# A pre-norm MoE, attention, MoE block: token lists compared in 16 bits, first gathers and first weight splits moved, first layer by slot halves

## The reference, cut to what matters

```
x = x + 0.5 * ffn(layernorm(x), Wg, w1, w2)
x = x + attention(layernorm(x), w_qkv, w_o)      # 16 heads, causal
x = x + 0.5 * ffn(layernorm(x), Wg, w1, w2)

def ffn(x):                                       # x: 2048 tokens x 256
    probs = softmax(x @ Wg); gates, experts = top_k(probs, 2)
    pos = position of each (token, choice) pair in its expert's list, kept = pos < C
    dispatched = x[list of each expert]           # 8 experts x C slots
    h = relu(dispatched @ w1)                     # 256 -> 1024
    out = h @ w2                                  # 1024 -> 256
    return sum over the two choices of gate * out, back at the token's row
```

## Time and profile before

| what | value |
|---|---|
| time, median of 3 runs (lowest, highest) | 876.12 us (874.57, 880.39) |
| profiled execution: span, first to last instruction | 872.3 us |
| busy in that span: PE, PEld, DVE, ACT, POOL | 88%, 77%, 52%, 42%, 36% |
| mean granted TensorE clock | 0.948 of full |
| first phase: list begins, first layer begins | 37.86 us, 60.21 us |
| third phase begins, list begins, first layer begins | 577.9 us, 605.22 us, 628.65 us |

### The profile page before, as it was taken

One profiled execution on the slowest core, in us unless ns is written; L12 is line 12 of the kernel. 1 busy time (PEld: TensorE's weight loads), 2 busy tenths in 40 slices (PEclk: granted clock), 3 DMA queues, 4 the chain that ended last, 5 costly groups with the idle time before them and its releaser, 6 DMA issues. The chain is left out here.

```text
span 872.3 us, 15775 instructions
## 1 busy us (share of the span) xinstructions
PE 765.8 (88%) x6076; PEld 670.4 (77%) x6076; DVE 452.7 (52%) x848; ACT 369.6 (42%) x611; POOL 310.6 (36%) x363
## 2 busy tenths in 40 slices
PE   5789999999999558888788787776899999999995
PEld 3479999999999546555556554454699999999995
DVE  7755544544453056757655667256554445444630
ACT  4215534554453001546553646523154445444531
POOL 3164364446422452132221212201644644464223
PEclk9899999999999877889988999978999999999998
DMA  9334454245401223220121120052344542554112
GB/s 333 105 119 119 108 148 124 64 118 144 126 9 18 25 96 146 75 76 20 58 77 58 45 75 27 26 164 57 91 119 133 142 125 48 142 137 124 18 18 24
DMA packets 60070, 80.27 MB, mean 92 GB/s; under 512 B 11140, under 2 KB 46980, under 8 KB 59988
## 3 DMA queue, kind: packets, MB, share of 16 engines
q1 hardware_dynamic: 44660, 60.35, 20.6%
q0 software_dynamic: 15360, 19.23, 11.9%
HBM read 51.72 MB, written 19.01 MB: 81 GB/s over the span
## 5 line engine op out<-in xcount | busy, mean ns | idle before, releaser
L610 DVE SCALAR_TENSOR_TENSOR first_h_lo<-first_ps_h,first_h_hi 128x320 fp32r<-128x320 f32 x128 | 62.9, 492 | 104.5 <-ACT first_h_hi L469 104.5
L610 DVE SCALAR_TENSOR_TENSOR second_h_lo<-second_ps_h,second_h_hi 128x320 fp32r<-128x320 f32 x128 | 62.9, 491 | 104.6 <-ACT second_h_hi L469 104.6
L386 POOL DMA_INDIRECT after_first<-first_scaled,first_add_now x40 | 69.4, 1734 | 115.6 <-ACT first_scaled L462 113.0
L386 POOL DMA_INDIRECT out_dram<-second_scaled,second_add_now x40 | 69.2, 1729 | 116.1 <-ACT second_scaled L462 113.5
L1100 DVE TENSOR_REDUCE at_maxima<-at_ps_front 128x4 f32<-128x512 f32 (+2 forms) x96 | 96.3, 1038 | 15.9 <-PE at_ps_front L1228 15.4
L984 POOL TENSOR_SCALAR_AFFINE_SELECT at_probs<-at_probs 128x512 f32<-128x512 f32 x64 | 39.9, 635 | 170.8 <-ACT at_probs L1040 169.9
L1040 ACT ACTIVATE at_probs<-at_ps_keys 128x768 f32<-128x768 f32 (+1 forms) x96 | 81.6, 876 | 25.1 <-PE at_ps_keys L1259 23.5
L721 PE MATMUL first_ps_o<-first_w_hi,first_h_hi 128*128 128x256 f32 x320 | 91.2, 285 | 0.0
L721 PE MATMUL second_ps_o<-second_w_hi,second_h_hi 128*128 128x256 f32 x320 | 91.2, 285 | 0.0
L721 PE MATMUL first_ps_o<-first_w_lo,first_h_hi 128*128 128x256 f32 x320 | 90.0, 281 | 0.0
L721 PE MATMUL first_ps_o<-first_w_hi,first_h_lo 128*128 128x256 f32 x320 | 90.0, 281 | 0.0
(11 more groups left out here) (271 smaller groups left out, 1765.0 us busy)
## 6 DMA issues: line engine op xcount, KB each, us to landing
first_w_raw<-in_L_ffn_w_dram SPq DMA_DIRECT2D x16, 1024.0 KB, 8.6
second_w_raw<-in_L_ffn_w_dram SPq DMA_DIRECT2D x16, 1024.0 KB, 7.1
at_q_stack<-at_pre_hi SPq DMA_DIRECT2D x16, 256.0 KB, 2.4
at_k_stack<-at_pre_hi SPq DMA_DIRECT2D x16, 256.0 KB, 2.5
x<-_attn_hidden_states_dram SPq DMA_DIRECT2D x4, 512.0 KB, 5.6
normed_rows<-first_xn SPq DMA_DIRECT2D x4, 512.0 KB, 6.7
x<-after_first SPq DMA_DIRECT2D x4, 512.0 KB, 5.5
at_q_stack<-at_pre_lo SPq DMA_DIRECT2D x8, 256.0 KB, 2.6
```

The lines of the kernel that those rows point to most:

```text
L386: pool.indirect_dma_start(sum_rows, bass.IndirectOffsetOnAxis(ap=add_now[par][:, s:s + 1], axis=0), scaled[par][:, s, :], None, bounds_che ...
L610: v.scalar_tensor_tensor(h_lo[:, f, a * HALF:(a + 1) * HALF], ps_h[:, f % 2, a, 0:HALF], 0.0, h_hi[:, f, a * HALF:(a + 1) * HALF].bitcast( ...
```

## The change: what it does

1. `lane` and `slot_tile` become fp16 tables that repeat each number `PART` = 8 times (1024 and 320 elements a partition). `column` and `in_tile` are fp16. The sum that `column` was built in gets its own fp32 tile `base`.
2. In each part one comparison with two tensors makes all eight `of_lane` (128 lanes x 8 groups, the group innermost) in place of eight comparisons with a scalar; `of_tile` and `tokens_of` are laid out the same way, 40 x 8. A matmul of the list then reads its weights and its moving columns at a step of 8 fp16 elements. It waits once for the eight `of_lane` of a part.
3. The first two gathers read their rows from `gather_index` itself; the copy to `gather_now` and the wait for it stay for experts 2 to 7.
4. Expert 0's weight splits: in the first phase VectorE's w2 part moves to behind its w1 part, ahead of the logits. In the third phase VectorE makes high and low parts of both matrices behind the normalized rows, and ScalarE makes none. The loads of w1 and w2 signal separate semaphores.
5. The first layer goes over the slot halves outermost, hidden blocks inside. The first half waits for two batches of slots, the second for the third batch; waits for the PSUM banks are by single group; the second layer waits for the second half of a hidden block at slot tile 2.

```diff
-        self.lane = sb("lane", [P, P], F16)
-        self.slot_tile = sb("slot_tile", [P, LC])
+        self.lane = sb("lane", [P, P, PART], F16)
+        self.slot_tile = sb("slot_tile", [P, LC, PART], F16)
...
+        pool.iota(self.lane[:], [[1, P], [0, PART]], base=0, channel_multiplier=0, **small).then_inc(self.filled, 1)
+        pool.iota(self.slot_tile[:], [[1, LC], [0, PART]], base=0, channel_multiplier=0, **small).then_inc(self.filled, 1)
...
-                pool.tensor_tensor(tokens_of[:, part], of_tile[:, part],
-                                   token[:, part].unsqueeze(2).broadcast_to([P, PART, LC]), ALU.mult).then_inc(tokens_ready, 1)
+                pool.tensor_tensor(tokens_of[:, h], of_tile[:, h],
+                                   token[:, part].unsqueeze(1).broadcast_to([P, LC, PART]), ALU.mult).then_inc(tokens_ready, 1)
...
-            gather(0, 0)
-            gather(1, 1)
+            gather_rows(0, gather_index[:, 0:ST])
+            gather_rows(1, gather_index[:, ST:2 * ST])
...
-            if not first_phase:                       # ScalarE
-                split_w1(0, 0)
-                split_w2(0, 0)
...
             if first_phase:                           # VectorE, behind norm.rows
                 split_w1(0, 0)
+                split_w2(0, 0)
+            else:
+                v.wait_ge(w1_loaded, 16)
+                v.tensor_copy(w1_hi[0][:], w1_raw[:]).then_inc(w_hi_done, 1)
+                split_w1(0, 0)
+                v.wait_ge(w2_loaded, 16)
+                v.tensor_copy(w2_hi[0][:], w2_raw[:]).then_inc(w_hi_done, 1)
+                split_w2(0, 0)
...
-            for n in range(K * T):
-                if n % PART == 0:
-                    part = slice(n, n + PART)
-                    v.tensor_tensor(of_tile[:, part], const.slot_tile[:].unsqueeze(1).broadcast_to([P, PART, LC]),
-                                    column[:, part].unsqueeze(2).broadcast_to([P, PART, LC]), ALU.is_equal).then_inc(tiles_ready, 1)
-                v.tensor_scalar(of_lane[:, n, :], const.lane[:], in_tile[:, n:n + 1], None, ALU.is_equal).then_inc(lane_ready, 1)
+            for h in range(PARTS):
+                part = slice(h * PART, (h + 1) * PART)
+                v.tensor_tensor(of_tile[:, h], const.slot_tile[:], column[:, part].unsqueeze(1).broadcast_to([P, LC, PART]),
+                                ALU.is_equal).then_inc(tiles_ready, 1)
+                v.tensor_tensor(of_lane[:, h], const.lane[:], in_tile[:, part].unsqueeze(1).broadcast_to([P, P, PART]),
+                                ALU.is_equal).then_inc(lane_ready, 1)
...
-            if not first_phase:                       # VectorE, behind the list
-                split_w1(0, 0)
-            split_w2(0, 0)
...
-                if n % PART == 0:                     # TensorE, list
-                    pe.wait_ge(tokens_ready, n // PART + 1)
-                pe.wait_ge(lane_ready, n + 1)
-                last = pe.matmul(ps_x[:, 1, 0:LC], of_lane[:, n, :], tokens_of[:, n, :], start=(n == 0), stop=(n == K * T - 1))
+                h, i = n // PART, n % PART
+                if i == 0:
+                    pe.wait_ge(lane_ready, h + 1)
+                    pe.wait_ge(tokens_ready, h + 1)
+                last = pe.matmul(ps_x[:, 1, 0:LC], of_lane[:, h, :, i], tokens_of[:, h, :, i], start=(n == 0),
+                                 stop=(n == K * T - 1))
...
-                pe.wait_ge(x_split, len(XB) * (e + 1) + 2)
-                for f in range(FT):
-                    pe.wait_ge(h_split, 2 * (FT * e + f + 1))
-                    fs = slice(f * P, (f + 1) * P)
-                    for a in range(2):
-                        cs = slice(a * HALF, (a + 1) * HALF)
+                for a in range(2):
+                    pe.wait_ge(x_split, len(XB) * e + 2 + (2 if a == 0 else 3))
+                    cs = slice(a * HALF, (a + 1) * HALF)
+                    for f in range(FT):
+                        n = FT * a + f
+                        pe.wait_ge(h_split, 2 * FT * e + n + 1)
+                        fs = slice(f * P, (f + 1) * P)
...
-                        if s == 0:
-                            pe.wait_ge(h_split, 2 * (FT * e + f + 3))
+                        if s in (0, 2):
+                            pe.wait_ge(h_split, 2 * FT * e + 4 + FT * (s // 2) + f + 1)
```

More of the change, by code:

```diff
@@ L31 @@
 ROW = D + E
+PARTS = 4
+PART = K * T // PARTS
 class Chain:
@@ L268, in feed_forward @@
             position = eb("position", [P, K * T])
-            column = eb("column", [P, K * T])
+            base = eb("base", [P, K * T])
+            column = eb("column", [P, K * T], F16)
             tile_no = eb("tile_no", [P, K * T])
-            in_tile = eb("in_tile", [P, K * T])
+            in_tile = eb("in_tile", [P, K * T], F16)
             numbers = eb("numbers", [P, LC])
-            of_tile = eb("of_tile", [P, K * T, LC], F16)
-            tokens_of = eb("tokens_of", [P, K * T, LC], F16)
-            of_lane = eb("of_lane", [P, K * T, P], F16)
+            of_tile = eb("of_tile", [P, PARTS, LC, PART], F16)
+            tokens_of = eb("tokens_of", [P, PARTS, LC, PART], F16)
+            of_lane = eb("of_lane", [P, PARTS, P, PART], F16)
         h_hi = sb("h_hi", [P, FT, CAP], F32R)
@@ L369, in _, with gather_rows @@
             last_row = pool.to_reg(TOK - 1)
[L371 to L375, removed]
+            def gather_rows(par, index):
                 for b, (s0, n) in enumerate(XB):
@@ L378, in gather @@
                         pool.indirect_dma_start(xg[par][:, s, :], None, xn_rows,
-                                                bass.IndirectOffsetOnAxis(ap=gather_now[par][:, s:s + 1], axis=0)
+                                                bass.IndirectOffsetOnAxis(ap=index[:, s:s + 1], axis=0)
                                                 ).then_inc(gathered[par][b], 16)
+            def gather(e, par):
+                pool.tensor_copy(gather_now[par][:], gather_index[:, bass.ds(e * ST, ST)]).then_inc(staged, 1)
+                pool.wait_ge(staged, e - 1)
+                pool.sem_inc(turn, 1)
+                gather_rows(par, gather_now[par])
             def add_out(e, par):
@@ L422, in split_w1 @@
             def split_w1(e, par):
-                act.wait_ge(raw_loaded, 32 * (e + 1))
+                act.wait_ge(w1_loaded, 16 * (e + 1))
                 act.activation(w1_hi[par][:], w1_raw[:], ACT.Copy).then_inc(w_hi_done, 1)
             def split_w2(e, par):
+                act.wait_ge(w2_loaded, 16 * (e + 1))
                 act.activation(w2_hi[par][:], w2_raw[:], ACT.Copy).then_inc(w_hi_done, 1)
@@ L466, in expert @@
                 for n in range(2 * FT):
-                    f, a = n // 2, n % 2
+                    a, f = n // FT, n % FT
                     act.wait_ge(h_made, 2 * FT * e + n + 1)
-                    act.activation(h_hi[:, f, a * HALF:(a + 1) * HALF], ps_h[:, f % 2, a, 0:HALF], ACT.Relu).then_inc(h_hi_done, 1)
+                    act.activation(h_hi[:, f, a * HALF:(a + 1) * HALF], ps_h[:, n // 2 % 2, n % 2, 0:HALF], ACT.Relu).then_inc(h_hi_done, 1)
                 if not last:
@@ L480, in expert @@
                     scale(e, par, s)
-            act.wait_ge(staged, 1)
             act.sem_inc(o_scaled, 2)
@@ L557, in _ @@
             chain(v.reduce_sum(position[:], product[:].rearrange("p k t e -> p (k t) e"), AX_X),
-                  v.reduce_sum(column[:], start[:].rearrange("p k t e -> p (k t) e"), AX_X),
+                  v.reduce_sum(base[:], start[:].rearrange("p k t e -> p (k t) e"), AX_X),
                   v.reciprocal(best[:], best[:]))
@@ L565, in _ @@
             chain(v.scalar_tensor_tensor(tile_no[:], position[:], float(2 * P), tile_no[:], ALU.is_ge, ALU.add),
-                  v.tensor_tensor(column[:], column[:], over[:], ALU.add))
+                  v.tensor_tensor(base[:], base[:], over[:], ALU.add))
             for a in range(3, ST):
@@ L569, in _ @@
             chain(v.scalar_tensor_tensor(in_tile[:], tile_no[:], -float(P), position[:], ALU.mult, ALU.add),
[L570 to L576 removed]
+                  v.tensor_tensor(column[:], base[:], tile_no[:], ALU.add))
+            for h in range(PARTS):
[4 more added lines that the diff above has]
+                                ALU.is_equal).then_inc(lane_ready, 1)
             v.wait_ge(list_made, 1)
@@ L708, in expert @@
                         parts += [(w1_lo[par][:, k, fs], xt_hi[:, k, cs]) for k in range(DK)]
-                        for n, (w, m) in enumerate(parts):
-                            last = pe.matmul(ps_h[:, f % 2, a, 0:HALF], w, m, start=(n == 0), stop=(n == len(parts) - 1))
+                        for m_no, (w, m) in enumerate(parts):
+                            last = pe.matmul(ps_h[:, n // 2 % 2, n % 2, 0:HALF], w, m, start=(m_no == 0),
+                                             stop=(m_no == len(parts) - 1))
                         last.then_inc(h_made, 1)
```

19 lines of the change are left out of this document (8 added, 11 removed).

## The result

The changed kernel takes 865.31 us (median of 4 runs, 862.16 to 866.90) against 876.18 (4 runs) before: ratio 0.988, 95% interval 0.985 to 0.991. The forecast was 867.0 in 864.5 to 872.5. The profiled execution spans 863.9 us against 872.3 (863.2 was forecast).

The account below looks back on a forecast made before the run. TensorE alone bounds the experts; from list to first layer VectorE, POOL and transfers also bound it, twice. Gains 0.9 + 0.9 + 3.1 + 4.2 = 9.1 us take the span from 872.3 to 863.2; plus 3.8, 867.0 us, range 864.5 to 872.5.

Parts of the forecast that it names:

- The gathers, held by the splits: List to first layer: VectorE's weight splits slow the first gathers (2.55, 2.50 us); with splits moved, each takes 0.96.
- M: Start of the 60 constant matmuls that end the list, at 47.01 in the first phase, 614.37 in the third.
- The list paced by TensorE at half clock: In the list, TensorE needs 2.25 us a part, VectorE and POOL about 1.6; gain 0.9 us a phase.
- 72 ns from one list matmul to the next: List matmuls with strided weights keep the 72 ns step (0.58/8); the sum adds nothing for strided loads.
- the rival of a costlier load: List matmuls: strided load takes twice as long, 144 ns, 4.6 us given back, 871.6 us; chance 0.18.
- M to first layer, 10.1: First layer begins 10.1 us behind the list's closing constant matmuls (range 9.6 to 10.5); gains 3.1 and 4.2 us.
- the fifth gather's 3.77: Before the first layer: the fifth gather's rows come at most 3.77 us behind its start, as before the change.
- The new order: First layer needs two batches split, so the wait of 1.02 us for the third split goes.
- The tables: POOL's tables grow by 896 and 280 elements, 1.2 us more, delaying TensorE's opening matmuls by 0.1 at most.
- the cover named for it: TensorE idles 1.13 us for normalized rows behind its ten opening matmuls, which hides the larger tables' delay.
- In experts 1 to 7 gain nothing: Later experts: the new first-layer order moves no wait of TensorE's, so cost and gain are nothing.
- The median run stands 3.8 above the span: Whole kernel: 3.8 us added to the forecast span of 863.2 gives the forecast time, 867.0.

Follow-up runs that it names:

- the five traces of this list: Changed kernel, and it with splits back, first-layer order back, distinct rows for empty slots, or padding: ratios 0.988, 0.992, 0.989, 0.987, 0.992 to the kernel before.

## Why the prediction was right, and where it was not

- **The gathers, held by the splits:** right. First gather at M + 1.33 and 1.31 (1.30 forecast), 1.17 and 1.10 us long, then 0.96; in the third phase the splits' return brings the 2.9 and 1.8 back, in the first the 2.9.
- **The list paced by TensorE at half clock:** right in the third phase (gain 0.9), short in the first (0.4; between nothing and 0.7 in the five traces of this list). There the third part's constants still took 1.37 us and not 1.03: I had put the clock's rise where it was before, and the granted clock was 0.50 until 45.2 where it had risen near 44.4.
- **"72 ns from one list matmul to the next":** a misreading that came out even, by luck. In the kernel before, the last matmuls of that row followed VectorE's comparisons. Contiguous ones follow each other in 29 ns at the full clock, and in the kernel before itself those that had no comparison to wait for did so in 33 to 36 ns at the half clock. The strided reading costs some 47 ns a matmul (76 to 78 in the changed kernel), so the rival of a costlier load was true in part as a mechanism, and my base was already too high by about as much. The rival's price of 144 ns was not reached. The Trainium skill ("SBUF — State Buffer", Specifications (TRN2)) says that each cross to a new 16-byte line pays a penalty; the trace agrees, 148 ns a load against 100.
- **M to first layer, 10.1:** measured 10.95 and 10.60, 0.45 and 0.1 beyond the upper bound of 10.5 I gave. I took the fifth gather's 3.77 as the high end and expected less. It stayed, 3.96 and 3.74, because of the repeated row. Its start also came later, at M + 6.59 and 6.47 and not 6.3, since the first gather takes 1.17 and 1.10 and not 0.96.
- **The new order:** right on the wait (1.06 us). It also takes away the idle time behind which the old order lost the clock, once in eight first layers.
- **The tables:** 2.2 us on POOL, not 1.2 (the large IOTA took 1.94); the cover named for it held, the list starts at 37.79 against 37.86. The splits ahead of the third phase's logits ended with 2.25 us to spare, copies at 1.22.
- **"In experts 1 to 7 gain nothing":** the order does gain nothing, but the step left out what larger tables do to addresses: 2.5 us. It more than made up for the 1.9 by which the stretches from list to first layer fell short; the stretch with attention then took 1.4 back. So it is luck that the sum (9.1 forecast, 8.4 in the span) looks better than its terms.
- **"The median run stands 3.8 above the span":** not a property of the kernel. The changed kernel's profiled run took 865.67 us, 1.8 above its own span of 863.9, and its three others are 1.7 or 1.8 above theirs, as are the runs of the kernel before whose span is on record. The rest of the 3.8 came from setting the span of one run beside the median of several. The time came out 1.7 below the forecast while the span was 0.7 above it.

Open: which address the pitch depends on, and what else decides it from one expert to the next. Only the shifts of 2272 and 2304 bytes were tried on purpose; the fp32 tables make a third.

## What to carry to other kernels

A pace read off a row belongs to whatever was late in it: before putting a duration into a sum, ask which engine the matmuls were following. When two engines have the same pace, speeding one up shows nothing until the other is dealt with: the list stood at 9.15 us with the clock alone improved, at 8.78 and 8.27 with the comparisons alone, and at 6.9 with both. A table that grows moves every address behind it, so compare with a padded kernel before crediting the edit.

## What the runs showed of the hardware

- Gathers of 128 rows of which most are the same row land late: 3.4 to 4.1 us behind the issue's start, against 2.7 to 2.8 with distinct rows.
- The second layer of the even experts (fp32, 256 columns) has two paces, 113.3 and 117.8 ns a matmul, and unused bytes in front of its operands change how many experts run at which.
- Weight loads at a step of 16 bytes last 148 ns, contiguous 96 to 100. Matmuls of 40 columns with weights and columns at that step follow at 76 ns, contiguous ones at 29.
- A stretch in which TensorE was busy 0.84 of 2 us was followed by the half clock in one list, 0.76 of 2 us in one first layer. But behind 0.49 of 2 us the clock stayed at full in another first layer, and behind 1.85 of 2 us or more it fell to half once.
